# Two of layer 2's eight contraction tiles as three fp32r products of halves, with weight edges split on the way in

## The reference

```python
x = x + x @ W.T + 0.5 * (x @ loraA[label]) @ loraB.T          # layer 0, one W for all batches
x = x + dequant(round(x / d[i]) ...)    # layer 1: i from 8 thresholds on |x|, 8 scales d
x = x + x @ W2[adapter].T               # layer 2: a 1024x1024 weight chosen for each batch
x = x + (x @ B3[adapter].T) @ A3[adapter].T                    # layer 3, rank 16
```

## Time and profile before

| | us |
|---|---|
| median of 3 runs (463.9 to 465.26) | 464.14 |
| the profiled execution, its own time | 464.56 |
| its span in the trace | 462.7 |
| PE busy | 454.7 (98%) |
| DVE busy | 415.4 (90%) |
| ACT busy | 326.7 (71%) |
| POOL busy | 8.1 (2%) |
| all DMA queues, mean rate | 149 GB/s |

### The profile page before, as it was taken

The page is one execution under the profiler, slowest core; times in us unless marked ns, Lnnn a source line. Parts: engine busy times, 40 slices in busy tenths (PEclk is TensorE's granted clock), DMA queues, the critical chain, the costliest instruction groups (busy, mean ns, idle before and its releaser), DMA issues.

```text
span 462.7 us, 7306 instructions
## 1 busy us (share of the span) xinstructions
PE 454.7 (98%) x3006; PEld 410.9 (89%) x3006; DVE 415.4 (90%) x395; ACT 326.7 (71%) x274; POOL 8.1 (2%) x18
## 2 busy tenths in 40 slices
PE   7999999999999999999999999999999999999995
PEld 7899999889998899889998899989998899988884
DVE  4889999999699996999699996999869999999983
ACT  5699979958398747967398754996349848665730
POOL 1000000000000000000000000100000000000000
PEclk9999999999999999999999999999999999999999
DMA  7983430557128534367227543183322522245242
GB/s 279 343 334 104 91 103 1 91 188 279 69 92 221 196 142 159 69 204 279 76 91 188 197 174 126 48 261 132 120 92 91 181 92 96 75 173 180 94 159 91
DMA packets 17941, 69.15 MB, mean 149 GB/s; under 512 B 2421, under 2 KB 3445, under 8 KB 13045
## 3 DMA queue, kind: packets, MB, share of 16 engines
q1 hardware_dynamic: 17044, 62.41, 37.5%
q0 software_dynamic: 864, 6.29, 7.3%
HBM read 54.01 MB, written 8.39 MB: 135 GB/s over the span
## 4 chain that ended last, share of the span: by engine, by line
PE 90%; DMA 3%; issue 2%; DVE 2%; SPq 2%; ACT 1%; DVEq 0%; ACTq 0%
PE l_ps L838 39%; PE l_ps L773 37%; PE l_ps L853 6%; PE bx_ps L872 2%; PE l_ps L783 2%; DMA w_sb<-w 2%; PE bx_ps L799 2%; DMA adapter_ids<-adapters 1%; PE l_ps L902 1%; PE bx_ps L806 1%; PE bx_ps L879 1%; DVE quant L628 1%; ACT cand L439 0%; ACT magnitude L429 0%; SPq L287 0%
## 5 line engine op out<-in xcount | busy, mean ns | idle before, releaser
L838 PE MATMUL l_ps<-x,w_sb 128*128 128x256 f32 x896 | 196.9, 380 | 0.4 <-DVE x L595 0.4
L838 PEld LDWEIGHTS l_ps<-x,w_sb 128*128 128x128 f32 x896 | 169.2, 190 | 25.3 <-issue 2.8
L634 DVE COPY_PREDICATED quant<-mask,cand 128x2048 f32<-128x2048 int8 (+2 forms) x77 | 145.6, 1891 | 0.4
L439 ACT ACTIVATE cand<-x,inv_delta 128x2048 f32<-128x2048 f32 (+2 forms) x88 | 134.5, 1528 | 8.8 <-DVE quant L628 7.0
L449 ACT ACTIVATE mask<-magnitude,thr_bias 128x2048 fp8e5<-128x2048 f32 (+2 forms) x77 | 117.7, 1529 | 13.4 <-DVE quant L634 12.7
L608 DVE TENSOR_SCALAR cand<-cand,delta 128x2048 f32<-128x2048 f32 (+2 forms) x88 | 87.9, 999 | 10.1 <-ACT cand L439 9.8
L616 DVE TENSOR_SCALAR cand<-cand,lower,upper 128x2048 f32<-128x2048 f32 (+2 forms) x88 | 93.4, 1062 | 0.4
L773 PE MATMUL l_ps<-x_hi,w_hi 128*128 128x256 f32 x512 | 87.1, 292 | 0.9 <-DVE x_lo L565 0.9
L773 PE MATMUL l_ps<-x_hi,w_lo 128*128 128x256 f32 x512 | 82.8, 283 | 0.0
L773 PE MATMUL l_ps<-x_lo,w_hi 128*128 128x256 f32 x512 | 82.5, 283 | 0.0
L773 PEld LDWEIGHTS l_ps<-x_hi,w_hi 128*128 128x128 f32 x512 | 71.4, 191 | 6.6 <-issue 4.2
(11 more groups left out here) (66 smaller groups left out, 231.0 us busy)
## 6 DMA issues: line engine op xcount, KB each, us to landing
w_sb<-w SPq DMA_DIRECT2D x31, 1024.0 KB, 4.9
out<-x SPq DMA_DIRECT2D x32, 256.0 KB, 2.2
x_raw<-x SPq DMA_DIRECT2D x15, 512.0 KB, 6.4
x_lo<-x_raw POOLq DMA_DIRECT2D x6, 1024.0 KB, 8.2
a_raw<-a SPq DMA_DIRECT2D x8, 512.0 KB, 3.6
w_sb<-w SPq DMA_DIRECT2D x7, 512.0 KB, 7.4
b_sb<-b SPq DMA_DIRECT2D x8, 256.0 KB, 2.7
a_raw<-a SPq DMA_DIRECT2D x8, 128.0 KB, 6.3
```

The lines of the kernel that those rows point to most:

```text
L439: act.activation(cand[:, c % CANDS, 0:n], x2_unit(u), ACT.Identity, bias=ROUND, scale=inv_delta[:, k:k + 1]).then_inc(rounded, 1)
L634: dve.copy_predicated(y, mask[:, m % MASKS, 0:n].bitcast(I8), t).then_inc(merged, 1)
L838: last = nc.tensor.matmul(l2_bank(b, q)[:, i * S:(i + 1) * S], w2_tile(b, o)[:, k * P:(k + 1) * P], x2[:, b % SLOTS, k * S:(k + 1) * S], s ...
```

## The change

In layer 2 of batches 0 to 6 (`SPLIT` = 7), the contraction tiles k = 0 and 1 (`EDGE` = 2) go as three fp32r matmuls each; k = 2 to 7 stay float32. Batch 7 stays float32 throughout.

The weights are loaded in two kinds of piece. The six float32 blocks of an output tile are one DMA of 384 KB into a ring of four. The two edge blocks of two output tiles are one DMA of 256 KB, and two such pairs are held raw. ACT copies a pair into `w2_hi` and, with the sign turned, into `w2_lo`; a POOL DMA adds the raw pair to `w2_lo`. There are three places for split pairs (`HALVES` = 6 tiles). Pairs 0, 1 and 2 of batch s are split in step s, one step before PE uses them; pair 3 is split in the step of its use. DVE makes `x2_hi` and `x2_lo` of the first two tiles of x2 after each `quantise`.

To make room, layer 0's weights are staged in the candidate buffers, `low_parts`, `bx_parts` and `fold` share one buffer, layer 3's `a3` is loaded into the second half of `x3` once the stores out of it have landed, `b3` is held without its zero columns, and batch 7's weights lie in halves of buffers that its smaller units leave free. Semaphores are counted anew: `l2_done` now counts output tiles, `w2_used` counts tiles of the ring.

```diff
-CHUNKS = 3
+EDGE = 2
+SPLIT = B - 1
+EW = EDGE * P
+EX = EDGE * S
+RING = 4
+RAW = 4
+HALVES = 6
...
-        w2_sb = sb("w2_sb", [P, CHUNKS, 2, T * P], F32)
+        w2_sb = sb("w2_sb", [P, RING, T * P - EW], F32)
+        w2_edge = sb("w2_edge", [P, RAW, EW], F32)
+        w2_hi = sb("w2_hi", [P, HALVES, EW], F32R)
+        w2_lo = sb("w2_lo", [P, HALVES, EW], F32R)
+        x2_hi = sb("x2_hi", [P, EX], F32R)
+        x2_lo = sb("x2_lo", [P, EX], F32R)
...
+        def raw_edges(q):
+            return w2_edge[:, 2 * q % RAW:2 * q % RAW + 2, :]
+        def split_pair(tiles, b, q):
+            first = 2 * (4 * b + q) % HALVES
+            return tiles[:, first:first + 2, :]
+        def a3_raw(b):
+            return x3[:, HW:BW] if b < B - 1 else w2_edge[:, :, :].rearrange("p o w -> p (o w)")[:, 0:D]
...
+            def load_w2(b, o, adapter):
+                n = T * b + o
+                if b == B - 1 and o >= RING:
+                    sp.wait_ge(x2_done, LAST)
+                elif n >= RING:
+                    sp.wait_ge(w2_used, n - RING + 1)
+                sp.dma_start(w2_tile(b, o), w2[bass.ds(adapter, 1), o, :, EW:T * P].rearrange("l p w -> p (l w)"))\
+                  .then_inc(w2_loaded[o] if b < B - 1 else last_w2_loaded[o], 16)
+            def load_edges(b, q, adapter):
+                n = 4 * b + q
+                if n >= 2:
+                    sp.wait_ge(w2_added[(n - 2) % 4], 16 * ((n - 2) // 4 + 1))
+                sp.dma_start(raw_edges(q), w2[bass.ds(adapter, 1), 2 * q:2 * q + 2, :, 0:EW]
+                             .rearrange("l o p w -> p (l o) w")).then_inc(w2_edge_loaded[q], 16)
...
+            def load_b3(b, adapter):
+                if b < B - 1:
+                    if b > 0:
+                        sp.wait_ge(bx_done, b)
+                    dst, src = b3_sb[:, :], b3
+                else:
+                    sp.wait_ge(x2_done, LAST)
+                    dst, src = magnitude[:, HW:HW + T * 2 * QUAD], b3_wide
+                sp.dma_start(dst, src[bass.ds(adapter, 1)].rearrange("l p w -> p (l w)"))\
+                  .then_inc(b3_loaded, 16)
+            def load_a3(b, adapter):
                 if b == 0:
                     sp.wait_ge(b0_split_done, 1)
-                else:
-                    sp.wait_ge(bx_done, b)
-                    sp.wait_ge(a3_split_done, b)
-                sp.dma_start(b3_sb[:, :, :].rearrange("p k r -> p (k r)"),
-                             b3[bass.ds(adapter, 1)].rearrange("l p w -> p (l w)")).then_inc(b3_loaded, 16)
-                sp.dma_start(a3_raw[:, :], a3[bass.ds(adapter, 1)].rearrange("l r w -> r (l w)"))\
+                elif b < B - 1:
+                    sp.wait_ge(out_stored[2], 16 * b)
+                    sp.wait_ge(out_stored[3], 16 * b)
+                else:
+                    sp.wait_ge(w2_added[3], 16 * b)
+                    sp.wait_ge(w2_added[2], 16 * b)
+                sp.dma_start(a3_raw(b), a3[bass.ds(adapter, 1)].rearrange("l r w -> r (l w)"))\
                   .then_inc(a3_loaded, 16)
...
+            for q in range(2, 4):
+                load_edges(0, q, adapter)
+            for s in range(1, B):
+                adapter, last_adapter = adapter_of(s), adapter
+                if s < B - 1:
+                    load_edges(s, 0, adapter)
+                for o in range(RING, T):
+                    load_w2(s - 1, o, last_adapter)
+                if s < B - 1:
+                    load_w2(s, 0, adapter)
+                    if s + 3 < B:
+                        load_batch(s + 3)
+                    load_edges(s, 1, adapter)
+                    load_w2(s, 1, adapter)
+                    load_w2(s, 2, adapter)
+                    load_edges(s, 2, adapter)
+                    load_w2(s, 3, adapter)
+                    load_edges(s, 3, adapter)
+                else:
+                    for o in range(RING):
+                        load_last_edge(o, adapter)
+                    for o in range(RING, T):
+                        load_w2(s, o, adapter)
+                        load_last_edge(o, adapter)
+                    for o in range(RING):
+                        load_w2(s, o, adapter)
+                    load_a3(s, adapter)
...
+            def add_edges(b, q):
+                pool.wait_ge(w2_neg_done, 4 * b + q + 1)
+                pool.dma_start(split_pair(w2_lo, b, q), raw_edges(q), accum_op=ALU.add).then_inc(w2_added[q], 16)
+            add_x(2)
+            for q in range(3):
+                add_edges(0, q)
+            for s in range(1, B):
+                if s + 2 < B:
+                    add_x(s + 2)
+                add_edges(s - 1, 3)
+                if s < SPLIT:
+                    for q in range(3):
+                        add_edges(s, q)
...
+            def split_edges(b, q):
+                n = 4 * b + q
+                act.wait_ge(w2_edge_loaded[q], (b + 1) * 16)
+                if n >= HALVES // 2:
+                    act.wait_ge(l2_done, 2 * n - HALVES + 2)
+                act.activation(split_pair(w2_hi, b, q), raw_edges(q), ACT.Copy).then_inc(w2_hi_done, 1)
+                act.wait_ge(w2_hi_done, n + 1)
+                act.activation(split_pair(w2_lo, b, q), split_pair(w2_hi, b, q).bitcast(F32), ACT.Copy, scale=-1.0)\
+                   .then_inc(w2_neg_done, 1)
...
+                elif c < 2:
+                    act.wait_ge(w0_split_done, w0_pieces(4 + 2 * c))
...
+                    if j in (2, 3, 6):
+                        split_edges(0, (2, 3, 6).index(j))
...
-                    if j == 4 and s + 2 < B:
-                        low_rank_hi(s + 2)
+                    if j == 4:
+                        if s + 2 < B:
+                            low_rank_hi(s + 2)
+                        if s < SPLIT:
+                            split_edges(s, 0)
                     if j == 6:
                         drain_l0(s + 1, 0)
+                        if s < SPLIT:
+                            split_edges(s, 1)
                     if j == 7:
+                        if s < SPLIT:
+                            split_edges(s, 2)
                         drain_bx(s - 1)
...
+                    if j == 5:
+                        split_edges(s - 1, 3)
...
+                    if j == 3 and 0 < UNITS[u][0] < B - 1:
+                        split_edges(UNITS[u][0] - 1, 3)
...
-                dve.wait_ge(l2_done, b * 4 + q + 1)
+                dve.wait_ge(l2_done, T * b + 2 * q + 2)
...
+            def split_x2(b):
+                if b > 0:
+                    dve.wait_ge(l2_done, T * b)
+                dve.wait_ge(x2_done, x2_count(b))
+                dve.tensor_copy(x2_hi[:, :], x2[:, b % SLOTS, 0:EX]).then_inc(x2_hi_done, 1)
+                dve.wait_ge(x2_hi_done, b + 1)
+                dve.tensor_tensor(x2_lo[:, :], x2[:, b % SLOTS, 0:EX], x2_hi[:, :].bitcast(F32),
+                                  ALU.subtract).then_inc(x2_split_done, 1)
...
+                if UNITS[u][0] < SPLIT and u > 0:
+                    split_x2(UNITS[u][0])
...
             def layer2(b, q):
-                pe.wait_ge(w2_loaded[q], (b + 1) * 16)
                 if q == 0:
                     pe.wait_ge(x2_done, x2_count(b))
                     if b > 0:
                         pe.wait_ge(out_done, 4 * b - 1)
-                else:
-                    if q > 1:
-                        pe.wait_ge(x3_done, b * 4 + q - 1)
+                elif q > 1:
+                    pe.wait_ge(x3_done, b * 4 + q - 1)
                 for i in range(2):
                     o = 2 * q + i
-                    for k in range(T):
-                        last = nc.tensor.matmul(l2_bank(b, q)[:, i * S:(i + 1) * S], w2_tile(b, o)[:, k * P:(k + 1) * P],
-                                                x2[:, b % SLOTS, k * S:(k + 1) * S], start=(k == 0), stop=(k == T - 1))
-                last.then_inc(l2_done, 1)
+                    pe.wait_ge(w2_loaded[o], (b + 1) * 16)
+                    for k in range(EDGE, T):
+                        last = nc.tensor.matmul(l2_bank(b, q)[:, i * S:(i + 1) * S], w2_block(b, o, k),
+                                                x2[:, b % SLOTS, k * S:(k + 1) * S], start=(i == 0 and k == EDGE),
+                                                stop=False)
+                    last.then_inc(w2_used, 1)
+                if q == 0:
+                    pe.wait_ge(x2_split_done, b + 1)
+                pe.wait_ge(w2_added[q], 16 * (b + 1))
+                for i in range(2):
+                    hi = split_pair(w2_hi, b, q)[:, i, :]
+                    lo = split_pair(w2_lo, b, q)[:, i, :]
+                    for w, v in ((hi, x2_hi), (hi, x2_lo), (lo, x2_hi)):
+                        for k in range(EDGE):
+                            last = nc.tensor.matmul(l2_bank(b, q)[:, i * S:(i + 1) * S], w[:, k * P:(k + 1) * P],
+                                                    v[:, k * S:(k + 1) * S], start=False,
```

(31 more changed lines are left out.)

136 lines of the change are left out of this document (68 added, 68 removed).

## The result

| kernel | median us (lowest to highest, runs) | profiled execution | its span |
|---|---|---|---|
| before | 464.09 (463.9 to 465.58, 6) | 464.56 | 462.7 |
| changed | 459.8 (459.47 to 462.19, 6) | 459.77 | 458.0 |

The changed kernel takes 0.9908 of the time before (95% interval 0.9892 to 0.9923): 4.3 us faster, where 4.9 were forecast, and 459.8 us where 459.3 were. By the interval the gain is 3.6 to 5.0 us. The profiled execution, 459.77, lies on the 459.7 that the sum gave for it; the other five lie between 459.47 and 462.19, so that hit is closer than the method can promise.

A forecast was written before the change was run, and what follows sets the result against it. PE was taken to bound the kernel until layer 0 of batch 6 closes, then the chain of ACT and DVE. -5.85 + 0.1 + 0.85 = -4.9 us gave 459.7 for the profiled execution, 459.3 as median; range 457.2 to 462.4.

The forecast's parts named there:

- the anchor: Close of layer 0 of batch 6, at 341.46 us: before it PE sets the time, after it ACT and DVE.
- PE's products: Layer 2: each pair of output tiles 0.29 us less, 1.17 a batch, 8.2 over seven batches if all counted.
- Before the anchor: Batches 0 to 4, where PE leads: their cheaper products count in full, 5.85 us less.
- Step 1: First tile of batch 3 needs `drain_l0`, with 1.8 us to spare: 0 to 0.5 us of stall, taken as 0.1.
- The split of x2: DVE's added copy and subtraction in each step: 1.0 to 1.4 us, taken as 1.1, hidden in a steady step.
- After the anchor: Tail paced by ACT and DVE: PE stalls 1.6 us before `sum_bx` of batch 5; in all 0.85 us later.
- The moved DMAs: SP's more and smaller weight loads through the ring of four: hidden, bounded at 0 to 0.5 us.
- The load of `a3`: In step 6 it waits for stores to land: ACT stalls 2.1 us, taken as 0 in the sum.
- The adds: POOL's 28 adds of 256 KB: 2.2 to 9.1 us each to land, taken as about 4, hidden.
- PE the bound to the end: Rival: PE stays the bound throughout, so all of 8.2 us counts: 455.9 us; chance 0.07.
- ACT or DVE losing more in each step: Rival: new splits stall PE 0.3 to 0.5 us a step and the tail slips 0.5: 461 to 463; chance 0.27.
- The late loop: Rival: add and reload of raw pairs close too late for ACT's split before `drain_bx`: slower, 467 at 16.5 us; chance 0.11.

The follow-up runs named there:

- the second profile: The changed kernel run once more with nothing changed, as the measure for three kernels beside it: 459.8 us, 458.0 of it the span.

## Why the prediction was right

The mechanism was right: the gain counts up to the anchor, and behind it `drain_bx` of batch 5 and then of batch 6 hold PE back. That the two stretches came out within 0.04 and 0.20 us is partly luck, as said below.

- *PE's products.* 5.18 and 1.43 us for 12 and 12 matmuls are 0.432 and 0.119 each; about 0.3 a pair, as forecast, and no cost of switching. Steps fell by 1.19.
- *Before the anchor.* -5.71 of -5.75. Float32 edges with all the rest kept left the anchor where it was, which shows that the splits, adds and moved DMAs are covered there. The close agreement is luck in part: layer 2 of batch 0 started 0.14 us sooner (80.61 against 80.75), which the sum didn't have, and step 1 lost more than its 0.1. Other versions with the same code have their anchor up to 0.8 sooner.
- *Step 1.* Forecast 0.1, at most 0.5. In the changed kernel the next tile starts at 114.94 instead of 114.68, so 0.26 us are lost, and 0.1 more behind it. The forecast had put that tile at 116.17 in the kernel before; the timeline has it at 116.00, so 0.17 of its 1.8 us to spare weren't there. Two other profiles have brackets of 0.35 and 0.47 at this place, and with one product it is 3.8: the place was right, the size too small.
- *The split of x2.* 0.42 and 0.69 in place of an estimated 1.1, and the run of DVE 1.0 longer.
- *After the anchor.* +1.05 of +0.85, and +1.41 in the second profile. At `sum_bx` of batch 5 PE loses 1.63, bracket 1.47, of 1.6. Two experiments show it: with the copy moved ahead the wait is gone, and with PE's gain taken away it goes straight on the end. At that of batch 6 the bracket is 0.37 where 1.0 was forecast. The sum held all the same, since in the first profile that instruction comes when ACT's copy comes, 1.12 late against 1.1 forecast. The rest of the wait had been spent earlier, on a weight tile (0.25 by its bracket) and on the restarts behind the waits.
- *The term that was mis-sized.* The moved DMAs, bounded at 0 to 0.5 and taken as 0, hid a tile that came 0.25 to 2.44 us late in three profiles. It costs nothing only while `drain_bx` is later still, and in the second profile of the changed kernel it wasn't: the tile set the end there. PE waiting for a weight tile was one of the prediction's own signs of being wrong, and it did occur; it was too small to move the result out of the range, and it is part of why 4.3 us came and not 4.9.
- *The load of `a3`.* ACT's wait for it is 0.35, not 2.1: the load landed 0.5 sooner after the anchor and ACT came 1.2 later. The sum had it at 0 and didn't suffer.
- *The adds.* 4.7 us, within 2.2 to 9.1 and near the 4 taken. POOL issues them in a median of 869 ns with DVE busy 96% of a step; the longest is 1877 ns, where it was 1902 before. The Trainium skill (SBUF — State Buffer, section "SBUF: two separate sides") says that POOL can't write descriptors while DVE runs an operation that uses both of its ports. No such delay shows in the issues here. By the fit of the Trainium skill (DMA: Bandwidth & Descriptors, section "Anatomy of one DMA") 256 KB would be an estimated 2.6 us; the measured 4.7 is well above. Whether the adding itself or DVE's ports make the landings that long, no run here separates.
- *The rivals.* PE the bound to the end needed 455.9; the tail grew instead. ACT or DVE losing more in each step did not happen: the changed kernel has no wait of PE in steps 2 to 5. The late loop has 4.2 us to spare at the split that it feeds, by median landings. Its price, 0.8 to 1.3 a step for a loop just over its limit, was never tested at that size; at 13 to 15 us an add it was 10.7, several times what the same count gave for it.

## What to carry to other kernels

Find the instruction at which the bound passes from one engine to another, and keep two accounts. Work taken from the leading engine counts before that point and hardly behind it; work added to the followers counts behind it. Here 5.7 of 8.2 us came before it, and of the 2.3 behind it 0.2 to 0.6 counted. The best median (457.99 us, 0.9863 of before) came from moving two copies of 0.37 us on ACT, not from more savings on PE; two variants of it lie within 0.3 us. Where a wait disappears without a gain, look at the next wait of the same engine: here it grew from 0.37 to 0.91 when the wait for the tile went.
